# Two small-head attention layers: weighted values from 16-bit parts instead of fp32

## The reference, cut to what matters

```python
attn = softmax(q @ k.T * scale)          # per head, over 128 keys
out = einsum('bhqk,bhkd->bqhd', attn, v) # per head
y = out.reshape(b, s, 256) @ Wo + bias   # and x = x + y
```

## Time and profile before

| | us |
|---|---|
| median of 3 runs | 3235.36 (3233.37 to 3242.24) |
| profiled execution, first to last instruction (its span) | 3242.7 |
| `l0x`, one batch in steady state | 16.66 |
| `l2a`, one batch in steady state | 11.49 |

### The profile page before, as it was taken

The page is one execution under the profiler, slowest core; times in us unless marked ns, Lnnn a source line. Parts: engine busy times, 40 slices in busy tenths (PEclk is TensorE's granted clock), DMA queues, the critical chain, the costliest instruction groups (busy, mean ns, idle before and its releaser), DMA issues. The chain is left out here.

```text
span 3242.7 us, 71995 instructions
## 1 busy us (share of the span) xinstructions
PE 2896.7 (89%) x25739; PEld 2213.5 (68%) x25739; DVE 2254.9 (70%) x5484; ACT 1858.7 (57%) x3565; POOL 1714.4 (53%) x1824
## 2 busy tenths in 40 slices
PE   7969989798999886896787999899999799998898
PEld 5757765456888665674565555788888688887565
DVE  5567754665777632885786677677777677777787
ACT  3356753355666422564676555566666577775675
POOL 2122211223555355664773366788888588886800
PEclk9989999799999875897899999899999999999899
DMA  4010001000000444000002532000000000000100
GB/s 162 1 23 14 14 13 62 7 2 9 8 6 5 137 120 93 5 6 22 16 16 83 193 88 56 3 1 0 0 0 1 8 7 5 5 5 28 41 1 27
DMA packets 95167, 104.64 MB, mean 32 GB/s; under 512 B 40716, under 2 KB 82124, under 8 KB 91983
## 3 DMA queue, kind: packets, MB, share of 16 engines
q1 hardware_dynamic: 90328, 96.08, 9.6%
q0 software_dynamic: 4608, 5.57, 1.1%
HBM read 80.84 MB, written 13.71 MB: 29 GB/s over the span
## 5 line engine op out<-in xcount | busy, mean ns | idle before, releaser
L2232 PE MATMUL bank<-l3a_ln_xnT,far 128*128 128x128 f16 x3072 | 194.3, 220 | 1.8 <-POOL l3a_ln_xnT L2046 1.8
L2232 PEld LDWEIGHTS bank<-l3a_ln_xnT,far 128*128 128x128 f16 x3072 | 181.7, 99 | 3.3 <-POOL l3a_ln_xnT L2046 2.2
L877 PE MATMUL bank<-l2f_xnT,l2f_wi 128*128 128x512 f16 x672 | 157.0, 382 | 7.0 <-POOLq L741 6.4
L3542 PE MATMUL bank<-l0x_v,l0x_pT 128*128 128x128 f32 x1024 | 134.1, 279 | 3.2 <-ACT l0x_pT L3970 1.5
L3542 PEld LDWEIGHTS bank<-l0x_v,l0x_pT 128*128 128x128 f32 x1024 | 127.1, 192 | 13.8 <-issue 4.7
L1226 PE MATMUL bank<-l3f_xnT,near 128*128 128x512 f16 x480 | 120.2, 388 | 6.9 <-DVE l3f_xnT L1011 3.5
L3136 POOL TENSOR_TENSOR l1x_prob<-l1x_prob,l1x_srec 128x512 f32<-128x512 f32 x64 | 66.7, 1043 | 111.1 <-DVE l1x_srec L2905 111.1
L1241 PE MATMUL bank<-near,l3f_h 128*128 128x256 f16 x960 | 119.1, 274 | 5.3 <-DVE l3f_h L1016 2.4
L877 PEld LDWEIGHTS bank<-l2f_xnT,l2f_wi 128*128 128x128 f16 x672 | 65.4, 98 | 78.2 <-POOLq L741 9.9
L3048 ACT ACTIVATE l3x_prob<-bank,l3x_less,l3x_q_rr 128x128 f32<-128x128 f32 x256 | 96.5, 457 | 37.4 <-DVE l3x_less L2928 37.3
L1241 PEld LDWEIGHTS bank<-near,l3f_h 128*128 128x128 f16 x960 | 94.0, 98 | 34.6 <-DVE l3f_h L1016 4.0
(11 more groups left out here) (735 smaller groups left out, 9461.6 us busy)
## 6 DMA issues: line engine op xcount, KB each, us to landing
far<-in_l1f_in SPq DMA_DIRECT2D x32, 256.0 KB, 4.9
l2f_front<-l2f_shares SPq DMA_DIRECT2D x5, 1024.0 KB
sums<-near SPq DMA_DIRECT2D x2, 2176.0 KB, 18.8
far<-in_l1f_down SPq DMA_DIRECT2D x32, 128.0 KB, 5.2
far<-sums SPq DMA_DIRECT2D x8, 512.0 KB, 7.4
l2f_wi<-in_l2f_in SPq DMA_DIRECT2D x14, 256.0 KB, 6.2
far<-l0x_kT SPq DMA_DIRECT2D x64, 48.0 KB
far<-l2x_kT SPq DMA_DIRECT2D x32, 96.0 KB
```

The source lines that it names most:

```text
L877: last = nc.tensor.matmul(bank[:, :], wi16[n % 2][p][:, a, k, :], xnT[q][:, k, 512 * g:512 * g + 512], start=(k + p + q == 0), stop=(k == ...
L2232: last = nc.tensor.matmul(bank[:, P * j:P * j + P], w(k, 512 * c + P * j, P, p), norm.xnT[u][q][:, k, :], start=(k + p + q == 0), stop=(k ...
L3542: last = nc.tensor.matmul(b_o[:, at:at + P], pT[f % 3][:, j, :], v_all[b % NV][:, hv:hv + P], start=True, stop=True)
```

## The change

For the kinds "axial" and "grouped" ("halved"):

- `heads_out` takes the probabilities as two 16-bit parts: the upper halves of the fp32 words, read in place as bf16 (every second bf16 of the tile), and the fp32 remainder as fp16 in a new tile `p_lo`. The values are split alike into `v_all` and `v_lo`. Each head has four matmuls (both parts by both parts), each of W columns (9 or 17) in place of 128.
- POOL gets `lower_probs`, one 128 x 512 subtraction for each group of 4 heads, and `lower_values`, one subtraction for each batch (128 x 288 in `l0x`, 128 x 68 in `l2a`). Its order in a step changes: `lower_out` goes to the end of the step's subtractions, `add_bias` behind the probabilities.
- `heads_out` of a block runs a step later (two steps behind its scores). `pT` has UB + 2 buffers in place of 3, the values one buffer more.
- DVE's `keep_out` moves from the start of the odd step to behind `keep_max`, into the same step as the second half's `heads_out`. `upper_out` on ACT stays where it was.

```diff
+    NP = UB + 2 if halved else 3
+    BEHIND = 2 if halved else 1
...
                     for j in range(4):
                         h = head(g, u, j)
                         at = W * (h % (H // rounds))
                         hv = W * (h // 4 if kind == "grouped" else h)
-                        last = nc.tensor.matmul(b_o[:, at:at + P], pT[f % 3][:, j, :], v_all[b % NV][:, hv:hv + P],
-                                                start=True, stop=True)
+                        if halved:
+                            p2 = (pT[f % NP][:, :].bitcast(BF16)[:, 2 * P * j + 1:2 * P * (j + 1):2],
+                                  p_lo[f % NP][:, P * j:P * j + P])
+                            v2 = (v_all[b % NV][:, :].bitcast(BF16)[:, 2 * hv + 1:2 * (hv + W):2],
+                                  v_lo[b % NV][:, hv:hv + W])
+                            for n, (i, k) in enumerate(((0, 0), (0, 1), (1, 0), (1, 1))):
+                                last = nc.tensor.matmul(b_o[:, at:at + W], p2[i], v2[k], start=(n == 0), stop=(n == 3))
...
-                        if back is not None:
-                            heads_out(back, u)
+                        if out is not None:
+                            heads_out(out, u)
...
-                    if done is not None and (rounds > 1 or done % R == R - 1):
+                    if not halved and done is not None and (rounds > 1 or done % R == R - 1):
                         keep_out(done)
...
                     if new is not None:
                         keep_max(new)
+                    if halved and done is not None and done % R == R - 1:
+                        keep_out(done)
                     if new is not None and kind == "axial":
                         keep_also(new)
...
+                def lower_probs(g, u):
+                    f = UB * g + u
+                    pool.wait_ge(e_ready, f + 1)
+                    nc.gpsimd.tensor_tensor(p_lo[f % NP][:, :], pT[f % NP][:, :], pT[f % NP][:, :].bitcast(BF16)[:, 1::2],
+                                            ALU.subtract).then_inc(p_split, 1)
+
+                def lower_values(b):
+                    pool.wait_ge(v_kept, b + 1)
+                    nc.gpsimd.tensor_tensor(v_lo[b % NV][:, :], v_all[b % NV][:, 0:HV * W],
+                                            v_all[b % NV][:, 0:HV * W].bitcast(BF16)[:, 1::2], ALU.subtract
+                                            ).then_inc(v_split, 1)
...
+                    probs = block_of(s - 1) if halved else None
+                    if probs is not None:
+                        lower_probs(probs, 0)
                     if wg is not None:
                         rsqrt(wg)
+                    if probs is not None:
+                        lower_probs(probs, 1)
...
+                    if probs is not None:
+                        for u in range(2, UB):
+                            lower_probs(probs, u)
+                    if halved and ln is not None:
+                        add_bias(ln)
                     if halve_of(s) is not None:
                         lower_q(halve_of(s))
                     if ky is not None:
                         lower_k(ky)
+                    if halved and value_of(s - LATE) is not None:
+                        lower_values(value_of(s - LATE))
+                    if halved and cl is not None:
+                        lower_out(cl)
```

More of the change, by code:

```diff
@@ L3265, in small_attention_layer @@
     add_of = lambda s: batch_at(s - 2 * R - 2)
-    NZ, NK, NV = (3 if split else 2, 3, LEAD // 2 + 1) if R == 2 else (3, 3, 5)
+    halved = kind in ("axial", "grouped")
+    NZ, NK, NV = (3 if split else 2, 3, LEAD // 2 + 1 + halved) if R == 2 else (3, 3, 5)
+    NP = UB + 2 if halved else 3
+    BEHIND = 2 if halved else 1
     NZK = 2 if R == 2 else 3
@@ L3311, in small_attention_layer @@
             zq.append(room([H, SLOT], F16))
-        pT = [sb(f"pT{i}", [P, 4, P]) for i in range(3)]
+        pT = [sb(f"pT{i}", [P, 4 * P]) for i in range(NP)]
+        if halved:
+            p_lo = [sb(f"p_lo{i}", [P, 4 * P], F16) for i in range(NP)]
+            v_lo = [sb(f"v_lo{u}", [P, HV * W], F16) for u in range(NV)]
+            p_split, v_split = sem("p_split"), sem("v_split")
         smax = [sb(f"smax{u}", [P, parts, 4 * UB]) for u in range(2)]
@@ L3531, in heads_out @@
                         if g % R == 0:
-                            pe.wait_ge(v_kept, b + 1)
+                            pe.wait_ge(v_split if halved else v_kept, b + 1)
                         if split:
@@ L3536, in heads_out @@
                             after(pe, o_read, b)
-                    pe.wait_ge(e_ready, f + 1)
+                    pe.wait_ge(p_split if halved else e_ready, f + 1)
                     for j in range(4):
@@ L3541, in heads_out @@
                         hv = W * (h // 4 if kind == "grouped" else h)
-                        last = nc.tensor.matmul(b_o[:, at:at + P], pT[f % 3][:, j, :], v_all[b % NV][:, hv:hv + P],
-                                                start=True, stop=True)
+                        if halved:
+                            p2 = (pT[f % NP][:, :].bitcast(BF16)[:, 2 * P * j + 1:2 * P * (j + 1):2],
[4 more added lines that the diff above has]
+                                last = nc.tensor.matmul(b_o[:, at:at + W], p2[i], v2[k], start=(n == 0), stop=(n == 3))
+                        else:
+                            last = nc.tensor.matmul(b_o[:, at:at + P], pT[f % NP][:, P * j:P * j + P],
+                                                    v_all[b % NV][:, hv:hv + P], start=True, stop=True)
                     last.then_inc(o_made, 1)
@@ L3566, in _ @@
                 for s in STEPS:
-                    new, back = block_of(s), block_of(s - 1)
+                    new, back, out = block_of(s), block_of(s - 1), block_of(s - BEHIND)
                     pj, kt, tn, fin = project_of(s), split_of(s), turn_of(s), finish_of(s)
@@ L3968, in exponentials @@
                     act.wait_ge(st_made, f + 1)
-                    after(act, o_made, f - 2)
-                    nc.scalar.activation(pT[f % 3][:, :, :].rearrange("p h k -> p (h k)"), b_st[f % 2][:, :], ACT.Exp,
-                                         scale=scale).then_inc(e_ready, 1)
+                    after(act, o_made, f - NP + 1)
+                    nc.scalar.activation(pT[f % NP][:, :], b_st[f % 2][:, :], ACT.Exp, scale=scale).then_inc(e_ready, 1)
                 def keep_values(b):
@@ L4146, in _ @@
                                                close_of(s))
+                    probs = block_of(s - 1) if halved else None
+                    if probs is not None:
+                        lower_probs(probs, 0)
                     if wg is not None:
                         rsqrt(wg)
+                    if probs is not None:
+                        lower_probs(probs, 1)
                     if s == STEPS[1]:
                         clear()
-                    if cl is not None:
+                    if not halved and cl is not None:
                         lower_out(cl)
-                    if ln is not None:
+                    if not halved and ln is not None:
                         add_bias(ln)
```

## The result

The kernel after the change takes 3302.8 us (median of 4 runs, 3300.9 to 3303.6), the one before 3234.9 in the same job: a ratio of 1.0197 with an interval of 1.0185 to 1.021, so 2.0% slower. The two medians lie 68 us apart (the ratio stands for 64), where the forecast said 37. The traced execution has a span of 3300.4 us against 3242.7 before, 58 us more (the one before was at the upper end of its runs). I count a stage from the start of its first `rstd` on POOL to the end of its last `lower_out`, in every trace in the same way: `l0x` went from 299.8 to 328.9 us and `l2a` from 212.5 to 245.9. That is +29 and +33, 62 together; all the rest of the trace is 5 us shorter.

The account below looks back on a forecast made before the run. PE was taken as the nearest bound, leaving the path after the change. `l0x` +17, `l2a` +24 and fill and drain -4 gave +37 on 3235, 3272 us; own range 3250 to 3295, whole range 3220 to 3306.

Parts of the forecast that it names:

- rival (d): PE falls to the lower clock after gaps ahead of `turn_again`: +40 us on top, 3312 us; chance 0.12.
- Heads on PE: On PE a group of 4 heads takes 0.46 us (upper bound 1.28) in place of 1.05, saving 0.59.
- lower_probs: POOL's new subtraction takes 1.16 us (1.04 to 1.27); POOL has 14.0 us per `l0x` batch, 12.0 in `l2a`.
- The hand-over: Odd to even step, `l0x`: ACT's queue waits behind `upper_out`; scores by key start 4.1 us after `keep_max`, 1.7 before.
- The rest of the even step: In `l0x`, scores by key to end of `keep_max`: 5.43 us less 2 x 0.59 for two head groups, 4.25.
- The blocks: DVE operations wait for POOL's instruction in flight: 2.3 us per batch in `l0x` (0 to 5.8), 1.1 in `l2a`.
- l2a: Batch of 13.1 us: odd part 4.35, even part 7.7, blocks 1.1; over 15 batches +24 us (+8 to +38).
- (a): Same chain, DVE's operations falling in POOL's gaps: `l0x` -17, `l2a` +8, 3222 us; chance 0.20.
- (b): PE's saving comes through, ACT's chain covered, both stages at DVE's floor: -49 and -10, 3176 us; chance 0.05.
- Fill and drain: Steps that only start or empty the two stages, paced by PE, get shorter: -4 us.

Follow-up runs that it names:

- queue edit: Kernel after the change, with `upper_out` moved on ACT behind `keep_q2T`: 3265.5 us, ratio to before 1.0086.
- The run without the block and with full clock: Kernel after, `upper_out` behind `keep_q2T`, probabilities' subtraction left out, unread matmuls ahead of `turn_again` (12/40 in `l0x`, 12/24 in `l2a`): 3209.8 us, ratio 0.9907.
- the fill: Kernel after, with unread matmuls on PE ahead of each `turn_again` (12/40 in `l0x`, 4/8 in `l2a`): 3290.7 us, ratio 1.0159.

## Why the prediction was right in direction and short by half

The measured 3303 us lies in the whole range of 3220 to 3306, but outside the forecast's own 3250 to 3295, and nearer to rival (d)'s 3312 than to 3272. The queue and the block were foreseen, and the runs show both. The sizes were not: +29 us for +17 in `l0x`, +33 for +24 in `l2a`, and some errors below cancel others.

**Heads on PE.** 0.40 us a group, not 0.46. The strided weight load costs nothing extra: 97 ns, beside 96 for the plain fp16 one, so its upper bound of 1.28 us a group played no part. The Trainium skill's figure of about 25 ns between starts ("TensorE: Matmul & The Clock Gate", Wait — 56ns, not 53.3ns?) is what the trace shows. The 0.06 us a group are too little to matter to the sum.

**lower_probs.** 1.06 us in the mean (1.03 to 1.31 in `l0x`), not 1.16; taken too long by a tenth. The mean lies within both bounds. The loss of some 0.4 us per meeting with DVE, which the prediction allowed POOL, is not seen: the median is 1.04 us and the longest 1.31. POOL is busy 12.8 us of an `l0x` batch (14.0 forecast) and 11.1 of 13.98 in `l2a` (12.0 forecast), 79%: the forecast that POOL would be over 85% busy and nearly a bound there was wrong, and so was the reason given why `l2a` can't become faster than now.

**The hand-over.** 3.9 us to the scores by key, forecast 4.1; ACT's wait of 3.99 us and PE's for `keep_oT` (1.09 us in the timeline) as described. The queue edit shows that it costs 29.5 us in `l0x`.

**The rest of the even step.** This is the first term that failed: "two groups of heads in the way save 2 x 0.59, so 4.25". It took 4.77 to the start of `keep_max` (380.85 to 385.62), 4.97 with a `keep_max` that isn't held. From the scores by key to the third group's scores it is 2.73 us, and before it was 2.70 (from 343.20, to 345.90): what the heads save there, matmuls at the lower clock give back. The stretch ahead of the first heads went from 1.76 us at a granted clock of 1.00 to 2.32 at 0.74, and the heads then save 0.53. Behind that, two row maxima of 0.69 us stand back to back on DVE, and the second saving ends at them. Then `keep_max` is held for 0.8. In the run without subtraction the even step is 9.5 us in most batches and the odd one 7.55, where I had 8.35 and 7.15; three quarters of the error are in the even step.

**The blocks.** I took 2.3 us a batch in `l0x`; the durations above sum to 2.3, but 0.4 of them is `lower_norm`'s. Which operations was partly wrong: the two adds carry 1.6 of it (held for 0.8 us each, not for half an instruction of 1.04), the two `keep_max` 0.4, `normalise` nothing. And a hold costs the batch less than it lasts: without the subtraction a steady batch is 17.06 us, so the block is worth 1.7. The sum for `l0x` was 15.5 + 2.3 = 17.8, the runs show 17.06 + 1.7 = 18.75: the chain was 1.6 us short and the block 0.6 too long, and these two errors partly cancel.

**l2a.** The chain without blocks was forecast as 4.35 + 7.7 = 12.05 us. The run without the block and with full clock has 12.05 too, but the equal sum is in part luck: from end to end of `keep_max`, as the forecast counts, its odd and even steps are 4.83 and 7.22 us (4.25 and 7.80 from start to start), and 0.57 of the odd one is a `keep_max` held beside the bias addition (0.76 us, 0.19 before), which the forecast didn't have.

Two terms were put at nothing here. One is the clock, which stood beside the sum as rival (d) with 0.12: odd steps of the kernel after take 5.01 us at a granted clock of 1.00 and 7.06 and 6.67 at 0.76 and 0.74, while the even step is 7.8 us in most batches. The other is the hand-over on ACT, counted in `l0x` alone; the queue edit takes 4.9 us off this stage. The blocks, with 1.1 us a batch from `normalise` and two `keep_max`, missed two products that are held longest. The kernel after, then before (1380 to 1460 us):

```profile
L3789 DVE TENSOR_TENSOR l2a_k_tok<-l2a_turnd,l2a_ss 128x64 f32<-128x64 f32 x6 | 6.4, 1067 | 0.0
L3782 DVE TENSOR_TENSOR l2a_ss<-l2a_rr,l2a_t_gain 128x20 f32<-128x20 f32 x6 | 4.4, 730 | 0.0
```

```profile
L3774 DVE TENSOR_TENSOR l2a_k_tok<-l2a_turnd,l2a_ss 128x64 f32<-128x64 f32 x6 | 1.3, 218 | 0.0
L3767 DVE TENSOR_TENSOR l2a_ss<-l2a_rr,l2a_t_gain 128x20 f32<-128x20 f32 x7 | 1.3, 180 | 1.0
```

A batch is 13.98, 0.9 over the 13.1. As the subtraction cost this stage 10.8 us, 0.7 a batch, it is the chain that was too short.

What each loss is worth in `l2a`: the subtraction 10.8 us alone and 19.8 once queue and clock are mended, the queue 4.9 to 6.5, the clock 3.2 to 10.6 (net of what the fill costs). 5.5 us (218.0 against 212.5) remain without any of the three: from end to end of `keep_max` the even step is 7.22 us against 6.81 before, longer by less than the 0.9 forecast for `keep_out`, and the odd one 4.83 against 4.68, with the held `keep_max`.

**Rival (d)** was right that the clock falls in both layers (0.80 to 0.84 and 0.91 to 0.92 in windows of 40 to 50 us), and no run shows its 40 us. In `l0x` the fill gave back 0.9 us net in the kernel after and 1.6 in the one without the two other losses; what the clock alone costs there stays open, since the fill lengthens the odd steps. **Rivals (a) and (b)**: without the subtraction and with the old queue order the whole is still 3267, not 3222, so (a) was too cheap, by 18 us in `l0x` and 15 in `l2a`; (b), that PE's saving comes through once ACT's chain is gone, needs the block gone too, and then gives 34 us in `l0x` and a loss of 16 in `l2a`.

**Fill and drain.** The first `lower_out` of `l0x` starts at 247.8 us where it started at 238.7, so filling the stage takes longer, not less. Of these 9 us only 3.7 are there at the fourth `keep_max` (and 2.8 at that of `l2a`); the rest is `lower_out`'s later place in its step. For the filling the term of -4 us had the wrong sign. What lies outside the two stages is 5 us shorter, which says nothing: in the fourteen traces that part is 2719 to 2732 us long, 2730 before and 2726 after.

## What to carry to other kernels

When an engine is 93% busy and another 75%, don't count on more from the first than the difference, and only if nothing is added to the path between them: write down for each step which engine's chain ends last, and add to it the queue order, the block and the clock, since each of the three can eat the saving alone. A consumer moved behind a producer in one queue takes with it everything that other engines keep behind it in theirs; move the copy whose reader comes latest to the end of its queue. Ahead of work on GpSimd that reads SBUF, look for VectorE's operations with two SBUF operands, and give them one in the bank; here that shortened the odd step, but with PE's matmuls at the lower clock the stage gained nothing, and the two together weren't tried. A fill of matmuls can delay what stands behind it, so measure it by steps and not by the whole time alone.

## What was not expected of the hardware

- bf16 weights read in place, as every second 16-bit word of an fp32 tile, load in 97 ns like contiguous fp16 ones (96), and the matmuls follow each other at 0.025 us.
- A 128 x 256 add with both operands in SBUF takes up to 1.28 us beside GpSimd subtractions and 0.425 beside GpSimd writes of zeros that keep it as busy; with one operand in the bank it takes 0.425 beside the subtractions too.
- A one-operand cast of 128 x 16 (0.20 us) is held also by GpSimd's writes of zeros, up to 0.59 us, and not by GpSimd's power of 3.8 us on 128 x 20: a `keep_max` inside it takes 0.19.
- PE idle for 2.3 of 7.8 us is followed by an odd step at a granted clock of 0.71; with 128 x 128 matmuls in that time it runs at 1.00 and takes 1.6 us less. The stage gained 10.6 us by it, but 3.2 where the subtraction stood beside it.
